# One power a step, one statistics group a step, three second dispatches a step, and the first expert tiles' preparation moved ahead

## The reference

```python
def _L0_gnn_ref(x, adjacency, epsilon, W1, b1, rms_weight, W2, b2):
    neighbor_sum = jnp.einsum('bnm,bmd->bnd', adjacency, x)
    agg = epsilon * x + neighbor_sum
    h = jnp.einsum('bnd,dh->bnh', agg, W1) + b1
    h = jax.nn.silu(_rmsnorm(h, rms_weight))
    out = jnp.einsum('bnh,hd->bnd', h, W2) + b2
...
def _L0_ffn_ref(x, Wg, bg, W1, b1, W2, b2):
    gate_logits = xf @ Wg + bg
    top_w, top_i = jax.lax.top_k(gate_logits, TOP_K)
    top_w = jax.nn.softmax(top_w, axis=-1)
...
    for e in range(E):
        h = jax.nn.gelu(xf @ W1[e] + b1[e], approximate=False)
        out = out + w_dense[:, e:e + 1] * (h @ W2[e] + b2[e])
...
x = x + _L0_gnn_ref(_layernorm(x, axis=-1), adj, ...)
x = x + _L0_ffn_ref(_layernorm(x, axis=-1), ...)
```

## Time and profile before

| | us |
|---|---|
| Median of 3 runs | 526.97 (526.31 to 528.96) |
| The profiled execution, its own time | 527.95 |
| Its span, first to last instruction | 526.1 |
| TensorE busy in the span | 476.7 (91%) |
| VectorE busy | 348.6 (66%) |
| GpSimd busy | 364.5 (69%) |
| ScalarE busy | 262.2 (50%) |
| Mean granted TensorE clock | 0.966 of full |

### The profile page before, as it was taken

How to read it: one execution, slowest core, us unless ns; L and a number is a source line. 1 busy time by engine, 2 the same in 40 slices (tenths; PEclk the granted TensorE clock), 3 DMA queues, 4 the chain that set the end, 5 groups by cost and what they waited for, 6 DMA issues and landing times. The chain is left out here.

```text
span 526.1 us, 14004 instructions
## 1 busy us (share of the span) xinstructions
PE 476.7 (91%) x3693; PEld 424.3 (81%) x3693; DVE 348.6 (66%) x1486; ACT 262.2 (50%) x812; POOL 364.5 (69%) x334
## 2 busy tenths in 40 slices
PE   3597899999999998958799999999999999999990
PEld 2473667777777776748799999999999999999990
DVE  5748787666666666655867766666666666666651
ACT  1122233222222222415577777777777777777770
POOL 2423368888888887777777765555568888888884
PEclk9886999999999999978999999999999999999996
DMA  7991012222222221223344332222235555555430
GB/s 249 372 294 31 31 53 73 73 72 78 63 68 62 68 78 43 68 64 79 96 109 113 106 97 77 66 72 70 57 53 67 71 73 72 71 72 71 57 35 2
DMA packets 54577, 45.03 MB, mean 86 GB/s; under 512 B 9521, under 2 KB 46039, under 8 KB 54502
## 3 DMA queue, kind: packets, MB, share of 16 engines
q1 hardware_dynamic: 36480, 26.11, 18.3%
q0 software_dynamic: 16592, 17.13, 16.7%
q10 hardware_dynamic: 1430, 0.88, 0.5%
HBM read 25.75 MB, written 19.25 MB: 86 GB/s over the span
## 5 line engine op out<-in xcount | busy, mean ns | idle before, releaser
L703 ACT ACTIVATE gelu_t<-ps,block_w 128x128 f32<-128x128 f32 x568 | 162.7, 369 | 38.3 <-PE ps L605 38.3
L605 PE MATMUL ps<-slot_t,block_w 128*128 128x128 f32 x1136 | 152.3, 278 | 4.2 <-ACT slot_t L697 4.1
L391 POOL DMA_INDIRECT dispatched_rows<-payload,row_idx x128 | 128.7, 1006 | 36.0 <-issue 33.1
L620 PE MATMUL ps<-experts,gelu_t 128*128 x1136 | 151.5, 277 | 0.5 <-ACT gelu_t L703 0.5
L605 PEld LDWEIGHTS ps<-slot_t,block_w 128*128 128x128 f32 x1136 | 139.8, 194 | 5.4 <-ACT slot_t L697 5.4
L620 PEld LDWEIGHTS ps<-experts,gelu_t 128*128 128x128 f32 x1136 | 139.1, 193 | 1.0 <-issue 0.9
L403 POOL DMA_INDIRECT out_y<-y_out,slot_rows x71 | 112.8, 1588 | 23.7 <-issue 21.3
L400 POOL DMA_INDIRECT out_y<-y_out,slot_rows x71 | 70.7, 996 | 46.0 <-DVE y_out L990 36.9
L983 DVE TENSOR_TENSOR y_bias<-ps,block_w 128x128 f32<-128x128 f32 x142 | 41.5, 292 | 85.2 <-PE ps L620 84.2
L971 DVE COPY block_w<-experts 128x644 f32 x142 | 70.7, 498 | 1.4 <-issue 1.2
L530 PE MATMUL ps<-w2e,hidden 128*128 128x136 f32 x512 | 67.1, 279 | 0.0
(11 more groups left out here) (135 smaller groups left out, 447.8 us busy)
## 6 DMA issues: line engine op xcount, KB each, us to landing
slot_rows<-dispatched_rows SPq DMA_DIRECT2D x142, 66.5 KB
xs<-in_x SPq DMA_DIRECT2D x16, 256.0 KB, 7.4
xs_t<-in_x_t SPq DMA_DIRECT2D x16, 256.0 KB, 3.1
experts<-in_f_w SPq DMA_DIRECT2D x16, 256.0 KB, 5.1
out_y<-y_out,slot_rows POOLq DMA_INDIRECT x142, 3.3
adj_in<-in_adj_t SPq DMA_DIRECT2D x16, 128.0 KB, 5.0
dispatched_rows<-payload,row_idx POOLq DMA_INDIRECT x128, 2.4
dispatched_rows<-pad_rows SPq DMA_DIRECT2D x18, 66.5 KB
```

The costliest lines, as they stand in the source:

```text
L391: pool.indirect_dma_start(rows[k], bass.IndirectOffsetOnAxis(row_idx[:, g, j * TOP_K + k:j * TOP_K + k + 1], 0), payload[:, g * JT + j, 0: ...
L605: mm = pe.matmul(bank((2 * i + c // 2) % FH_BANKS, c % 2 * SLOTS, SLOTS), block_w[:, i % BLOCKS, c * P:(c + 1) * P], slot_t[:, i % 2, :], ...
L620: mm = pe.matmul(bank(Y_BANK + i % 2, 0, P), gelu_t[:, i % 2, c, :], experts[:, bass.ds(at + (OW2 + c * P), P)], start=(c == 0), stop=(c = ...
L703: act.activation(gelu_t[:, i % 2, c, :], ps[:, (2 * i + c // 2) % FH_BANKS, c % 2 * SLOTS:(c % 2 + 1) * SLOTS], ACT.Gelu, bias=block_w[:, ...
```

## The change

Four things are changed.

1. *One power a step.* `powers_in` and `powers` hold three strips of four numbers for each step: the mean square of group s + 1, the output's variance + eps of group s - 1, and the input's variance + eps of group s + 4. `pow_step(s)` raises all of them in one instruction over 12 numbers and waits for all three inputs. Since the inverse deviation no longer lands in `payload`, ScalarE copies it there ahead of its `tanh`, and each dispatch waits for that copy too (`rstd_stored`). The powers of groups 1 and 2, and of 3 and 4, are taken as one of 8 numbers each.
2. *The input's statistics one group a step* from group 5 on, in step s for group s + 5, where `STATS_AT` had up to three in one step.
3. *Three second dispatches a step* from step 3 on, in place of four. 42 of the 64 fall into the steps, 22 stand among the expert tiles, two in five.
4. *The order.* On TensorE the spread goes from the middle of the first layer to behind the second layer's first strip, the quadratic from behind the first layer to the second layer's third strip, and the sum of squares to the end of the step. On VectorE the mean square comes right behind the second norm, then the input's work, then gate, scaling and product. In step 15 the first two block copies and four `norm_slots` stand ahead of `place_rows(14)` and `second_norm(15)`.

```diff
-STATS_AT = {-4: (0,), -3: (1, 2), -2: (3, 4), -1: (5, 6), 0: (7, 8, 9), 1: (10, 11, 12), 2: (13, 14), 3: (15,)}
+STATS_AT = {-4: (0,), -3: (1, 2), -2: (3, 4)}
+
+STATS_FROM = 5
...
+        powers_in = sb("powers_in", [P, G + 1, 3, JT])
+        powers = sb("powers", [P, G + 1, 3, JT])
...
-        LATE_SECOND = G - 2
+        SECONDS_FROM = 3
+        SECONDS_LEFT = 3 * (G + 1 - SECONDS_FROM)
...
-            def pow_ln1(g):
-                pool.wait_ge(var1_ready, g + 1)
-                pool.tensor_tensor(rstd1[:, cols(g)], var1[:, cols(g)], neg_half[:],
-                                   ALU.pow).then_inc(rstd1_ready, 1)
-
-            def pow_ln2(g):
-                pool.wait_ge(var2_ready, g + 1)
-                pool.tensor_tensor(payload[:, cols(g), RSTD], var2[:, cols(g)], neg_half[:],
-                                   ALU.pow).then_inc(rstd2_ready, 1)
-
-            def pow_rms(g):
-                pool.wait_ge(ms_ready, g + 1)
-                pool.tensor_tensor(rrms[:, cols(g)], mean_sq[:, cols(g)], neg_half[:],
-                                   ALU.pow).then_inc(rrms_ready, 1)
+            def pow_ln1(groups):
+                first, last = groups[0], groups[-1]
+                pool.wait_ge(var1_ready, last + 1)
+                many = slice(first * JT, (last + 1) * JT)
+                pool.tensor_tensor(rstd1[:, many], var1[:, many], neg_half[:, 0:len(groups) * JT],
+                                   ALU.pow).then_inc(rstd1_ready, len(groups))
+
+            def pow_rms0():
+                pool.wait_ge(ms_ready, 1)
+                pool.tensor_tensor(rrms0[:], mean_sq0[:], neg_half[:, 0:JT], ALU.pow).then_inc(rrms_ready, 1)
+
+            def pow_step(s):
+                first = 0 if live(s + 1) else 1
+                last = 1 if s == 0 else 3 if live(s + STATS_FROM - 1) else 2
+                if first == 0:
+                    pool.wait_ge(ms_ready, s + 2)
+                if last > 1:
+                    pool.wait_ge(var2_ready, s)
+                if last > 2:
+                    pool.wait_ge(var1_ready, s + STATS_FROM)
+                pool.tensor_tensor(powers[:, s, first:last, :], powers_in[:, s, first:last, :],
+                                   neg_half[:, 0:(last - first) * JT].rearrange("p (a j) -> p a j", j=JT),
+                                   ALU.pow).then_inc(powers_ready, 1)
...
+                pool.wait_ge(rstd_stored, g + 1)
                 pool.indirect_dma_start(
                     rows[k], bass.IndirectOffsetOnAxis(row_idx[:, g, j * TOP_K + k:j * TOP_K + k + 1], 0),
                     payload[:, g * JT + j, 0:WID], None).then_inc(signal, 16)
+
+            def second(n):
+                dispatch(n // JT, n % JT, 1)
...
-                if live(s - 1):
-                    pow_ln2(s - 1)
+                if 0 <= s <= G:
+                    pow_step(s)
                 if live(s - 2):
                     dispatch(s - 2, 0, 0)
                     dispatch(s - 2, 1, 0)
-                if live(s - 3) and s - 3 < LATE_SECOND:
-                    dispatch(s - 3, 0, 1)
-                    dispatch(s - 3, 1, 1)
-                for g in STATS_AT.get(s, ()):
-                    pow_ln1(g)
-                if live(s + 2):
-                    pow_rms(s + 2)
+                if s >= SECONDS_FROM:
+                    second(3 * (s - SECONDS_FROM))
+                if s in STATS_AT:
+                    pow_ln1(STATS_AT[s])
+                if s == -2:
+                    pow_rms0()
                 if live(s - 2):
                     dispatch(s - 2, 2, 0)
                     dispatch(s - 2, 3, 0)
-                if live(s - 3) and s - 3 < LATE_SECOND:
-                    dispatch(s - 3, 2, 1)
-                    dispatch(s - 3, 3, 1)
-
+                if s >= SECONDS_FROM:
+                    second(3 * (s - SECONDS_FROM) + 1)
+                    second(3 * (s - SECONDS_FROM) + 2)
...
-                if i == LAST_RANKS + 1:
+                late = i - (LAST_RANKS + 2)
+                if late == -1:
                     for j in range(JT):
                         dispatch(G - 1, j, 0)
-                n = (i - LAST_RANKS - 4) // 3
-                if i % 3 == (LAST_RANKS + 4) % 3 and 0 <= n < (G - LATE_SECOND) * JT:
-                    dispatch(LATE_SECOND + n // JT, n % JT, 1)
+
+                n = SECONDS_LEFT + late // 5 * 2 + (late % 5 == 2)
+                if late >= 0 and late % 5 in (0, 2) and n < G * JT:
+                    second(n)
...
-                after(pe, prefix_used, g - 3)
+                after(pe, prefix_used, g - 2)
...
-                pe.wait_ge(rrms_ready, g + 1)
+                if g == 0:
+                    pe.wait_ge(rrms_ready, 1)
+                else:
+                    pe.wait_ge(powers_ready, g)
                 for j in range(JT):
-                    mm = pe.transpose(bank(QR_BANK, j * P, P),
-                                      rrms[:, g * JT + j:g * JT + j + 1].to_broadcast([P, P]), ident[:])
+                    mm = pe.transpose(bank(QR_BANK, j * P, P), rrms_of(g, j).to_broadcast([P, P]), ident[:])
...
-                pe.wait_ge(ms_ready, min(g + 4, G))
+                pe.wait_ge(ms_ready, min(g + 3, G))
...
-                elif live(s + 1):
-                    spread(s + 1)
                 first_layer(s, (2, 3))
-                if s > 0 and live(s + 2):
-                    quadratic(s + 2)
...
                 second_layer(s, 0)
+                if s > 0 and live(s + 1):
+                    spread(s + 1)
                 second_layer(s, 1)
                 if s == 0:
                     sum_squares(1)
-                elif live(s + 2):
-                    sum_squares(s + 2)
                 residual(s, 2)
                 second_layer(s, 2)
+                if s > 0 and live(s + 2):
+                    quadratic(s + 2)
                 residual(s, 3)
                 second_layer(s, 3).then_inc(l2_done, 1)
                 if live(s - 1):
                     prefix(s - 1)
                 if live(s + 3):
                     aggregate(s + 3)
+                if s > 0 and live(s + 2):
+                    sum_squares(s + 2)
...
+                act.copy(payload[:, cols(g), RSTD], powers[:, g + 1, 1, :]).then_inc(rstd_stored, 1)
                 act.activation(half_tanh[:, cols(g)], gap[:, cols(g)], ACT.Tanh, scale=0.5).then_inc(tanh_ready, 1)
 
...
 
             def norm1(g):
-                dve.wait_ge(rstd1_ready, g + 1)
...
                 after(dve, agg_done, g - 2)
                 for j in range(JT):
                     t = g * JT + j
...
-                dve.wait_ge(rstd2_ready, g + 1)
-                mine = payload[:, cols(g), :]
...
+            for s in range(-4, G):
+                if live(s - 1):
+                    second_norm(s - 1)
+                if s > 1 and live(s + 1):
+                    mean_square(s + 1)
+                if live(s + 3) and s > -3:
+                    norm1(s + 3)
+                if s > 0 and live(s + 4):
+                    place_adj(s + 4)
+                if s >= 0 and live(s + STATS_FROM):
+                    stats1_of(s + STATS_FROM)
...
+                if live(s - 1):
+                    gate_scores(s - 1)
+                if s > 0 and live(s + 1):
+                    scale_agg(s + 1)
+                if live(s - 1):
+                    gate_choice(s - 1)
...
+                if s > 0 and live(s + 2):
+                    product(s + 2)
...
+                if s == G - 1:
+
+                    copy_block(0, expert_of(dve, 0))
+                    copy_block(1, expert_of(dve, 1))
+                    for i in range(AHEAD):
+                        norm_slots(i)
+                if live(s - 1):
+                    place_rows(s - 1)
+                if s == EARLY_GROUPS:
+                    early_table()
...
-            copy_block(0, expert_of(dve, 0))
-            copy_block(1, expert_of(dve, 1))
+            second_norm(G - 1)
             at = expert_of(dve, 2)
-            for i in range(AHEAD):
-                norm_slots(i)
-            second_norm(G - 1)
```

89 lines of the change are left out of this document (44 added, 45 removed).

## The result

Before takes 527.25 us (median of 4 runs, 526.31 to 528.96), the changed kernel 507.0 us (4 runs, 505.42 to 510.12): a ratio of 0.962, 95% interval 0.957 to 0.967. The forecast was 513.0 (507.0 to 522.0), faster. The sign and the mechanism of the steps came true; the gain is 20.3 us where 14.0 were forecast, at the lowest end of the range. The profiled execution after took 506.98 us with a span of 505.2 (before 527.95 and 526.1).

What follows compares the result with a forecast made beforehand. GpSimd was taken to set steps 2 to 12, TensorE the expert tiles; -7.1 (steps 2 to 12) - 0.5 (step 13) - 1.9 (start) - 4.5 (passage) = -14.0 us, 526.97 to 513.0 us, range 507 to 522.

Steps and rivals of the forecast that it cites:

- floor: TensorE's own time for one graph-layer step, put together from trace pieces: 11.63 us.
- Steps 2 to 12: Graph-layer steps: TensorE's 11.63 us a step would set them, 127.9 us against 135.0, -7.1 us.
- So GpSimd sets these steps: Steps 2 to 12 before: GpSimd's 12.44 us a step sets the pace, TensorE next, 0.6 to 0.8 us behind.
- The wide power: GpSimd's merged power of 12 numbers a partition: taken as 1.6 us, between 1.04 and 3.1.
- the iota: A 128x64 GpSimd instruction of 0.27 us, the nearest row differing in size, used to put the merged power at 1.6 us.
- the point from which it decides: Length of the merged power up to which GpSimd's step stays under TensorE's 11.63 us: 2.6 us.
- x: Price of GpSimd's merged power of 12 numbers, shown by no row: taken as 1.6 us.
- The start: Steps 0 and 1: statistics one group a step remove waits, first groups come later; step 1 ends at 60.6, -1.9 us.
- the clock stays up: Rival in step 1: the clock doesn't fall, 4 us less, 509 us, the rest as forecast; chance 0.13.
- Step 13: Early table still ahead of the second norm, spread waits 2.0 us: 12.65 us against 13.2, -0.5 us.
- The passage: Step 15 to the expert tiles: earlier power of group 14, first expert layer at 11.6 us against 15.73, -4.5 us.
- The end: Stretch behind the expert tiles to the program's end: no term in the sum, forecast change 0.

Runs made afterwards that it cites:

- the run with three seconds a step: The kernel before with only its second dispatches cut to three a step, 22 left among the expert tiles: 588.8 us, ratio 1.032, on a chip of the slower kind.
- the run with three powers: The changed kernel with its one power of 12 numbers made as three powers of 4 in a row: 514.3 us, ratio 0.974.
- the run with two parts undone: The changed kernel with input statistics bunched at their old places and first blocks and slots prepared behind the last rows: 524.6 us, ratio 0.996.

## Why the prediction was right, and where it was off

The sign and the mechanism of the steps were right. That the measured 507.0 still lies in the range of 507.0 to 522.0 is luck: the lower end was drawn for a clock that stays up, and what led there was a floor that I had 2.1 us too high, a start and a passage each 1.9 us better than forecast, and 1.9 us at the end, which is in no term of the sum; step 13 took back 0.6.

**Steps 2 to 12 (-7.1, measured -9.1).** The mechanism held: GpSimd came under TensorE's floor, and TensorE sets the steps without a wait. The floor was mis-sized. I had put it together from pieces that begin behind a wait, 0.93 for the quadratic and 0.92 for the sum of squares; without waits they take 0.85 (134.84 to 135.69) and 0.81:

```profile
134.84 1.02 PE L519 MATMUL ps<-agg,quad 128*128 128x512 f32 x2
135.69 0.40 PE L551 MATMUL ps<-ident_wg,xs_t 128*128 128x136 f32 x2
...
138.04 0.95 PE L526 MATMUL ps<-ones,prod 128*128 128x1 f32 x8
138.85 0.68 PE L544 MATMUL ps<-agg_r,w1b 128*128 128x512 f32 x1
```

That is 0.19 us a step, 2.1 in eleven. "So GpSimd sets these steps" was true of steps 7 to 12 alone; in steps 3 to 6 the order bound, and the run with three seconds a step shows that relief alone would have stopped there. The rest, 0.6 us a step, needs the new order as well; no run where before takes 527 has the new order with the old dispatches, so what the order is worth alone is not shown.

**The wide power (1.6, measured 2.32).** The nearest row that I went by, the iota, was the wrong kin. It did no harm only because the point from which it decides, 2.6 (2.64 by the run with three powers: 11.44 - 8.80), was still above it. The rate of the Trainium skill ("GPSIMD Engine Reference", Elementwise — side-by-side cycle accounting), by which x would have been 1.06, does not hold here for a power, which took 2.32 us.

**The start (-1.9, measured -3.8).** Two terms were off, against each other. The first step begins 1.67 us later (29.49 against 27.82), not 0.85, mostly because the double powers take 1.70 us and not 1.1. And the low clock was the wrong reason for the old step 1: I had it hold until 53.0 and cost the new step as much. It fell for 3.41 us instead (0.50 from 45.46 to 48.87). The old step is slow whether or not the clock is: before with three seconds a step had 3.4 us of low clock in it, where before had 9.0, and still took 17.73 us against 18.43, with 4.0 us of waits of TensorE in place of 2.7 (window):

```profile
44.58:62.31 17.73, 13.72 (x80) 9.19 (x80) 15.82 (x95) 2.95 (x5) 9.26 (x9) 0.90 0.08 24
```

VectorE, busy for 15.82 us with three groups' statistics in the step, set it. The case "the clock stays up", 509 us at a chance of 0.13, came half true.

**Step 13 (-0.5, measured +0.1).** The wait at the spread is 1.62 us, near the 2.0 forecast with a shorter power; the 0.61 us at the sum of squares was missing.

**The passage (-4.5, measured -5.1 and -1.3).** The power is there 5.1 us into step 15 (1.51 us of wait, below), not 6, and the preparation then runs in the time in which VectorE would wait for the counts; the run with two parts undone prices it at 2.9 us. Timeline of VectorE after, against the earlier trace rows:

```profile
211.81 0.19 DVE L827 TENSOR_TENSOR scaled<-payload,powers 128x32 f32<-128x32 f32 x1 [1.51 <-POOL powers L403]
...
214.57 0.54 DVE L973 COPY block_w<-experts 128x644 f32 x1 [0.72 <-issue]
...
216.19 1.11 DVE L979 TENSOR_SCALAR slot_n<-slot_rows 128x128 f32<-128x128 f32 x4
```

Before, TensorE waited 4.18 us for the slots and the clock was low from 230.54 to 240.78; after, it waits 1.47 us and the clock stays up. That goes with 1.3 us less in the first nine tiles, but the run in which the low clock came back lost only 0.3 us there, so the clock isn't shown to be the cause.

**The end (0, measured -1.9)** was in no step of the sum. The last outputs start 1.85 us apart in both kernels, but the program ends 8.5 us after the start of the last one before, and 6.6 us after:

```profile
517.62 1.55 POOL L403 DMA_INDIRECT out_y<-y_out,slot_rows  x1 [0.30 <-issue]
```

```profile
498.55 1.55 POOL L429 DMA_INDIRECT out_y<-y_out,slot_rows  x1 [0.31 <-issue]
```

(spans of 526.1 and 505.2). It is 8.5 us in the two kernels with the old dispatch schedule, 6.6 in all with three seconds a step, the old kernel among them, and 4.8 with four. So the schedule of the dispatches causes it; how is open.

**What the runs leave open.** The changed kernel itself wasn't run where before takes 567 us. Kernels with one small edit of it lost 8 to 12 per cent there, and before with its dispatch schedule alone lost 3, so it most likely loses there too. The cause of the late signals is not shown either. One observation: the eight traces hold 6,243 to 6,790 recorded semaphore events, the six where before takes 527 hold 10,757 to 10,857 for the same programs or nearly so, so records were lost where signals were late. The Trainium skill ("NOTIFIC — the notification-queue block", Overflow: three behaviours, one of which stalls the engine) says that the block's internal pipeline holds back the engines that write records rather than lose any in it; whether this is at work here, and would be without a profile, no run shows.

## What to carry to other kernels

When several small instructions are merged into one, its inputs must all be ready early in the cycle: the merged power was worth 6.4 us with one group's statistics a step, and with the statistics bunched TensorE waited 2.21 us for it in step 1. Before crediting a cycle to the busiest engine, look for cycles in which that engine doesn't yet hold the others up: the four early steps of before, at 12.0 us beside a GpSimd that took 12.44, showed where relief alone would end. And measure a floor's pieces where they run back to back, not behind a wait.
